# Half of a softmax-weights product moved from fp32 to three fp16 products, with the splits on three engines

## The reference

```python
q, k, v = hidden_states @ Wq, encoder_hidden_states @ Wk, encoder_hidden_states @ Wv
logits = einsum('bhqd,bhkd->bhqk', q, k) * scale + col_bias   # two masked token columns
probs = softmax(logits, axis=-1)
out = einsum('bhqk,bhkd->bhqd', probs, v) @ Wo + bo + residual
```

## Time and profile before

| | us | share of the span |
|---|---|---|
| time, median of 3 runs | 3488.54 | |
| span of the profiled execution | 3487.1 | |
| TensorE busy | 3363.5 | 96% |
| VectorE busy | 2345.2 | 67% |
| GpSimd busy | 2182.3 | 63% |
| ScalarE busy | 1765.5 | 51% |

### The profile page before, as it was taken

One profiled execution on the slowest core, in us unless ns is written; L12 is line 12 of the kernel. 1 busy time (PEld: TensorE's weight loads), 2 busy tenths in 40 slices (PEclk: granted clock), 3 DMA queues, 4 the chain that ended last, 5 costly groups with the idle time before them and its releaser, 6 DMA issues.

```text
span 3487.1 us, 70163 instructions
## 1 busy us (share of the span) xinstructions
PE 3363.5 (96%) x27442; PEld 1543.5 (44%) x27442; DVE 2345.2 (67%) x4444; ACT 1765.5 (51%) x2230; POOL 2182.3 (63%) x1050
## 2 busy tenths in 40 slices
PE   7999999999997888889999999999999999999998
PEld 3444444444442322234444444444444444444443
DVE  6666766666666788856676666666666666666666
ACT  5444444444445677764444444444444444444444
POOL 6877777767641000028777777777787677767776
PEclk9999999999998999999999999999999999999999
DMA  4000000000000000000000000000000000000000
GB/s 153 3 10 11 1 10 10 10 1 9 6 10 12 8 12 17 17 1 10 10 9 3 10 11 1 10 10 10 1 10 10 1 10 10 10 1 10 3 1 25
DMA packets 50178, 42.10 MB, mean 12 GB/s; under 512 B 4928, under 2 KB 42176, under 8 KB 49856
## 3 DMA queue, kind: packets, MB, share of 16 engines
q1 hardware_dynamic: 49136, 37.08, 3.5%
q10 hardware_dynamic: 720, 0.53, 0.1%
HBM read 32.36 MB, written 2.10 MB: 10 GB/s over the span
## 4 chain that ended last, share of the span: by engine, by line
PE 90%; ACT 3%; DVE 2%; POOL 2%; issue 2%; DMA 0%; SPq 0%; ACTq 0%; POOLq 0%; DVEq 0%
PE ps_j L858 39%; PE ps_j L1047 19%; PE ps_st L1007 13%; PE ps_sm L941 6%; PE ps_st L992 3%; PE ps_j L1034 3%; ACT pt L1495 2%; PE ps_sm L1021 2%; POOL acc L712 2%; PE ps_j L1067 1%; PE ps_st L941 1%; PE ps_j L950 1%; PE ps_j L1083 1%; PE ps_j L1058 0%; DVE nmg L1925 0%
## 5 line engine op out<-in xcount | busy, mean ns | idle before, releaser
L712 POOL TENSOR_TENSOR acc<-acc,pt 128x1024 f32<-128x1024 f32 x570 | 1365.5, 2396 | 435.8 <-ACT pt L1495 381.6
L1495 ACT ACTIVATE pt<-ps_st 128x1024 f32<-128x1024 f32 x768 | 742.7, 1019 | 447.2 <-PE ps_st L1007 435.4
L1047 PE MATMUL ps_j<-pt,v 128*64 128x512 f32 x3040 | 694.3, 599 | 1.3 <-DVE q_l L1836 1.3
L1935 DVE CUSTOM_DVE_ANT_0 ps_sm<-ps_sm,bias_m,nmx 128x512 f32<-128x512 f32 x666 | 480.5, 757 | 271.1 <-PE ps_j L941 227.5
L858 PE MATMUL ps_j<-w_h,ctx_h 128*128 128x128 f16 x3072 | 532.3, 220 | 2.3 <-ACT rinv L1511 1.1
L858 PE MATMUL ps_j<-w_l,ctx_h 128*128 128x128 f16 x3072 | 531.2, 220 | 0.0
L858 PE MATMUL ps_j<-w_h,ctx_l 128*128 128x128 f16 x3072 | 531.2, 220 | 0.0
L1935 DVE CUSTOM_DVE_ANT_0 ps_sm<-ps_sm,bias_m 128x512 f32<-128x512 f32 x486 | 334.6, 707 | 198.7 <-PE ps_j L941 185.8
L733 POOL TENSOR_TENSOR o_un<-o_un,rinv 128x512 f32<-128x512 f32 x111 | 141.7, 1277 | 477.3 <-ACT rinv L1507 293.7
L1047 PEld LDWEIGHTS ps_j<-pt,v 128*64 128x64 f32 x3040 | 201.7, 136 | 407.6 <-issue 369.6
L1972 DVE RECIPROCAL rinv<-rinv 128x256 f32<-128x256 f32 x190 | 331.4, 1746 | 14.0 <-ACT rinv L1511 4.4
(11 more groups left out here) (186 smaller groups left out, 5477.2 us busy)
## 6 DMA issues: line engine op xcount, KB each, us to landing
w_raw<-wk SPq DMA_DIRECT2D x25, 256.0 KB, 2.8
pt<-ctx_t SPq DMA_DIRECT2D x6, 1024.0 KB, 7.2
w_raw<-wv SPq DMA_DIRECT2D x24, 256.0 KB, 3.7
wo_raw<-wo SPq DMA_DIRECT2D x28, 128.0 KB, 2.0
w_raw<-wq SPq DMA_DIRECT2D x24, 128.0 KB, 2.8
k_h<-k_l SPq DMA_DIRECT2D x72, 32.0 KB, 2.0
x<-x_t SPq DMA_DIRECT2D x4, 512.0 KB, 8.3
acc<-ctx_t SPq DMA_DIRECT2D x2, 1024.0 KB, 8.4
```

What stands on the lines that cost most here:

```text
L712: G.tensor_tensor(total, first, pt[:, n % RING, :], ALU.add).then_inc(s_acc, 1)
L1047: last = MM(dst[h * HD:(h + 1) * HD, :], values_of(p)[:, kt, h * HD:(h + 1) * HD], pt[:, (units(p) + kt) % RING, h * TQ:(h + 1) * TQ], sta ...
L1495: A(pt[:, n % RING, :], src.rearrange("p h q -> p (h q)"), ACT.Exp).then_inc(s_exp, 1)
L1935: last = V.tensor_tensor_reduce(out=src, in0=src, in1=bias_m[:, t, half * HALF:(half + 1) * HALF], scale=-1.0, scalar=nmx[:, 0, t, h:h + 1 ...
```

## The change

`thirds(p)` names 78 of the 96 wide items: 4 to 28, 52 to 77 and 84 to 110 (turned slots, without those in which the x splits of a layer's start are made). For these:

- `attend_in_thirds(p)` takes the place of `attend(p, 0)`. Key tiles 0 and 1 are multiplied in fp32 as before. Key tiles 2 and 3 are three fp16 products each, V high by P high, V rest by P high, V high by P rest, for two heads: 12 fp16 matmuls in place of 4 fp32 ones (8 instructions). `attend(p, 1)` stays.
- ScalarE makes `p_h` (fp16 of P, 1024 elements a partition) twice an item, one after `queries_hi` and one between the two `keys_hi`; and the first half of V becomes two instructions of 256 elements, `v_h` (fp16, key tiles 2 and 3) and `v32` (fp32, key tiles 0 and 1).
- GpSimd makes `p_l` = P - `p_h` twice an item (`weights_rest`), one ahead of `normalize`, one behind `output_lo`.
- VectorE makes `v_l` once an item (`values_lo`) out of PSUM, between `keys_lo` 1 and the reductions of block 2.
- The next user of the PSUM bank of V waits for `v_l` too. The DMA scratch of the compiler is set to 4096 bytes; the kernel issues no DMA from GpSimd.

```diff
@@ attend_in_thirds (new; called in turned_slot when thirds(s)) @@
+                pe.wait_ge(s_exp, units(p) + 2)
+                pe.wait_ge(s_v_sb, values_before(p) + 1)
+                dst = take("pva", p)
+                for kt in range(2):
+                    for h in range(2):
+                        MM(dst[h * HD:(h + 1) * HD, :], values_of(p)[:, kt, h * HD:(h + 1) * HD],
+                           pt[:, (units(p) + kt) % RING, h * TQ:(h + 1) * TQ], start=kt == 0, stop=False)
+                pe.wait_ge(s_v_l, thirds_before(p) + 1)
+                for i in range(2):
+                    pe.wait_ge(s_p_h, 2 * thirds_before(p) + i + 1)
+                    for n, (v, w) in enumerate(((v_h, p_h), (v_l, p_h), (v_h, p_l))):
+                        if n == 2:
+                            pe.wait_ge(s_p_l, 2 * thirds_before(p) + i + 1)
+                        for h in range(2):
+                            last = MM(dst[h * HD:(h + 1) * HD, :], v[:, p % 2, i, h * HD:(h + 1) * HD],
+                                      w[:, i, h * TQ:(h + 1) * TQ], start=False, stop=i == 1 and n == 2)
+                last.then_inc(s_pva, 1)
@@ scalar engine @@
+                if thirds(p) and not half:
+                    A(v_h[:, p % 2], src[:, 2:4], ACT.Copy, scale=VS / WS)
+                    src, to = src[:, 0:2], to[:, 0:2]
+                A(to, src, ACT.Copy, scale=VS / WS).then_inc(s_v_sb, 1)
...
+            def weights_hi_of(p, i):
+                n = units(p) + 2 + i
+                act.wait_ge(s_exp, n + 1)
+                reaches(act, s_pva, wides(p))
+                A(p_h[:, i, :], pt[:, n % RING, :], ACT.Copy).then_inc(s_p_h, 1)
@@ gpsimd @@
+            def weights_rest(p, i):
+                n = units(p) + 2 + i
+                pool.wait_ge(s_p_h, 2 * thirds_before(p) + i + 1)
+                G.tensor_tensor(p_l[:, i, :], pt[:, n % RING, :], p_h[:, i, :], ALU.subtract).then_inc(s_p_l, 1)
@@ vector engine, called after keys_lo(s + 2, 1) when thirds(s + 1) @@
+            def values_lo(p):
+                dve.wait_ge(s_v_sb, values_before(p) + 1)
+                src = bank("v0", p).rearrange("p (k d) -> p k d", k=4)
+                split_lo(v_l[:, p % 2], src[:, 2:4], VS / WS, v_h[:, p % 2]).then_inc(s_v_l, 1)
@@ take @@
+                        if before == "v0" and thirds(m):
+                            pe.wait_ge(s_v_l, thirds_before(m) + 1)
```

More of the change, by code:

```diff
@@ L200, in split_sums, with thirds, thirds_before @@
     return not grouped(p) and not G0 - 3 <= p < G0
+def thirds(p):
+    return turned(p) and all(not first - 2 <= p < first + B for first in (STARTS[layer] for layer in WIDE))
+def thirds_before(p):
+    return sum(thirds(q) for q in range(p))
 def splits(p):
@@ L384, in build @@
         pt = sb("pt", [P, RING, 2 * TQ], F32)
+        p_h = sb("p_h", [P, 2, 2 * TQ], F16)
+        p_l = sb("p_l", [P, 2, 2 * TQ], F16)
+        v_h = sb("v_h", [P, 2, 2, P], F16)
+        v_l = sb("v_l", [P, 2, 2, P], F16)
         acc = sb("acc", [P, 2, 2 * TQ], F32)
@@ L460, in build @@
         s_v_sb = sem("s_v_sb")
+        s_v_l = sem("s_v_l")
+        s_p_h = sem("s_p_h")
+        s_p_l = sem("s_p_l")
         s_max_mm = sem("s_max_mm")
@@ L786, in _ @@
                     normed_lo(rms_batch(s))
+                if thirds(s):
+                    weights_rest(s, 0)
                 if past:
@@ L789, in _ @@
                     output_lo(s - 1)
+                if thirds(s):
+                    weights_rest(s, 1)
                 if summing and not turned(s):
@@ L1049, in attend, with attend_in_thirds @@
                 last.then_inc(s_pvb if part else s_pva, 1)
+            def attend_in_thirds(p):
+                pe.wait_ge(s_exp, units(p) + 2)
[15 more added lines that the diff above has]
+                last.then_inc(s_pva, 1)
             def sums(p):
@@ L1239, in turned_slot @@
                     project_out(s - 1, 0)
-                attend(s, 0)
+                if thirds(s):
+                    attend_in_thirds(s)
+                else:
+                    attend(s, 0)
                 score_block(3)
@@ L1475, in values @@
                     reaches(act, s_pvb if half else s_pva, wides(p - 2) + 1 if p >= 2 else 0)
-                A(values_of(p)[:, half * 4:half * 4 + 4, :], bank(f"v{half}", p).rearrange("p (k d) -> p k d", k=4),
-                  ACT.Copy, scale=VS / WS).then_inc(s_v_sb, 1)
+                src, to = bank(f"v{half}", p).rearrange("p (k d) -> p k d", k=4), values_of(p)[:, half * 4:half * 4 + 4, :]
+                if thirds(p) and not half:
[7 more added lines that the diff above has]
+                A(p_h[:, i, :], pt[:, n % RING, :], ACT.Copy).then_inc(s_p_h, 1)
             def exponentials(p, j):
@@ L1702, in turned_slot @@
                     queries_hi(s + 2)
-                    if not splits_x(s):
-                        keys_hi(s + 2, 0)
+                if thirds(s):
+                    weights_hi_of(s, 0)
+                if far and not splits_x(s):
+                    keys_hi(s + 2, 0)
+                if thirds(s):
+                    weights_hi_of(s, 1)
+                if far:
                     keys_hi(s + 2, 1)
@@ L2117, in turned_slot @@
                     keys_lo(s + 2, 1)
+                if thirds(s + 1):
+                    values_lo(s + 1)
                 peak()
@@ L2294 @@
     arrays["norm_w"] = np.ascontiguousarray(get("L1_xattn_norm_w").reshape(CQ, P).T)
-    nc = bacc.Bacc("TRN2", target_bir_lowering=False, num_devices=1)
+    nc = bacc.Bacc("TRN2", target_bir_lowering=False, num_devices=1, dynamic_dma_scratch_size=4096)
     a = {k: nc.dram_tensor(k, v.shape, mybir.dt.from_np(v.dtype), kind="ExternalInput").ap()
```

## The result

The changed kernel takes 3470.02 us (median of 4 runs, 3468.71 to 3470.83) against 3488.63 us of the kernel before: a ratio of 0.9949, 95% interval 0.9935 to 0.9963. That is faster by 0.5%, 18.6 us; 23.5 us were forecast, and 3470 lies inside the range. The profiled execution has a span of 3468.4 us and a time of 3470.16.

A forecast was written before the change was run, and what follows sets the result against it. TensorE's list of work was taken to bound every wide slot. Terms of -33.5, +8 and +2 us sum to -23.5 us, taking the span from 3487.1 to 3463.6 and the median to 3465 us, range 3453 to 3487.

The forecast's parts named there:

- The bound: In wide slots, TensorE's list of work sets the length: it is busy 30.03 of 30.03 us.
- Term 1: First half of P V on TensorE: 3.59 to 3.16 us, -0.43 us an item, x 78 = -33.5 us.
- The five waits: Semaphore waits inside the new TensorE function: met early, costed at nothing, bounded by 0.1 us an item, 8 us.
- ScalarE: Two copies of P, 1.06 us each, hidden in 1.99 us waits; V in two parts 0.68 us, complete 0.08 us later.
- Term 2: VectorE's rest of V delays a block 2 reduction and the closing pair's second head: +0.10 us x 78 = +8 us.
- Term 3: Six slots where VectorE builds token rows: slower rest of P delays normalize and VectorE, 6 x 0.33 = +2 us.
- Cover lost: From GpSimd's first rest of P on, every further 0.1 us goes straight through o_h and V.
- rival 2: Slow first rest of P on GpSimd: gain gone from about 2.5 us on; at 3.0 us, 3529 us; chance 0.12.
- GpSimd goes from 21.6 to 25.9 us in a slot of 29.7: full, but no bound: GpSimd's work in a slot with two rests of P added: fuller, but not what sets the slot's length.
- wrong altogether: Signs in the trace against the whole prediction: TensorE waiting for p_l, for o_l, or for an exponential.
- Rival 1: VectorE's queue ahead of the closing pair costs much more than 0.1: 0.35 us a slot, 3484 us; chance 0.20.
- Rival 3: TensorE's half-array fp16 products do not hide weight loads: six loads add 0.6 us, 3512 us; chance 0.06.

The follow-up runs named there:

- the products alone: Changed kernel with split tiles zeroed once at the start, the splits in the slots and their waits left out: 3454.34 us, 0.9905 of the kernel before.
- the splits alone: Changed kernel with all splits made, but the first half of P V in fp32 again and ScalarE copying all of V: 3516.3 us, 1.0085 of the kernel before.
- the addition ahead of the normalization: Changed kernel plus an unused GpSimd subtraction of 192 elements between the first rest of P and the normalization: 3495.95 us, 1.0027 of the kernel before.
- the rest of V moved: Changed kernel with VectorE's rest of V between the two reductions of block 2 instead of ahead of them: 3458.41 us, 0.9919 of the kernel before.
- both edits: Changed kernel with item 110 left unsplit and the rest of V placed between the two reductions of block 2: 3456.4 us, 0.991 of the kernel before.

## Why the prediction was right, and where not

- **The number**: 18.6 us of the 23.5 forecast. The sum of the plain slots was right to 0.01 us a slot. What is missing in the profiled execution is slot 110 (4.4 us with its own share of the gain), slot 28 (1.1), four slots with 0.13 each (0.5), the slots where the splits begin (0.3) and the clock in layer 1 (1.0); the higher clock at the start gave 2.5 back. That last one is luck: by its own slots the change gave 17.3 us.
- **The bound**: right. TensorE's list sets a wide slot; the slot fell with it.
- **Term 1, -0.43 us an item**: right. 3.59 to 3.16 us in the trace, 0.42 a slot with the products alone. The five waits cost nothing.
- **ScalarE**: right. The two copies of P took 1.05 us each inside waits for TensorE; V in two parts took 0.66 us (0.68 assumed, 0.70 as an estimate from the figures of the Trainium skill, which stand in the section What ACT_TABLE_LOAD costs of ScalarE: Activation LUTs, not in the one that the prediction names).
- **Term 2, +0.10 us**: right in place and size. Moving one instruction on VectorE removed it; the splits alone, with 0.22 us more on ScalarE, gave 0.32.
- **Term 3**: the place was right, the size a little high: the six token slots lost 0.24 us more than plain ones, 0.33 were assumed, 1.4 us in place of 2. Without the rests of P they lost nothing.
- **"Cover lost: from the first rest on, every further 0.1 us goes straight through"**: too strict. V had 0.16 us to spare, because neighbours on ScalarE overlap and `normalize` was 0.23 us late in the slot (1988.25 - 1973.82 against 1997.96 - 1983.76), not 0.30. That is why 0.50 us brought 0.34, and it puts rival 2's point at a rest of about 2.6 us.
- **"GpSimd goes from 21.6 to 25.9 us in a slot of 29.7: full, but no bound"**: this step failed, for one slot in 78. It was worked out from a plain slot and carried over to all ("all 78 items have this slot", and the only exceptions that it goes on to name are the six token slots), but slot 110 has no Q and K projections; there GpSimd was the bound before the change already, and was given 2.1 us more, with a fall of the clock behind the wait. It gave back 4.1 us of a forecast 23.5. The row was to be had: TensorE's wait of 2.30 us for `o_l` at 3445.27. TensorE waiting for `o_l` is one of the prediction's own signs of being wrong altogether, and it came in this one slot. The 21.6 is a slip besides: the slot of the earlier trace rows has 20.97, and with two rests of 2.13 that makes 25.2; 25.06 was measured.
- **Rival 1** (0.3 us or more on VectorE) and **rival 2** (GpSimd): neither came true, and the splits only and the addition ahead of the normalization show that both mechanisms are real: 0.5 us more a slot on GpSimd made the kernel 0.3% slower than the one before (1.0027). **Rival 3** is out, with different weights in each half array: steps of 0.215 us. Each of the six pairs of loads lies beside the products before it. The rule named with it (TensorE: Matmul & The Clock Gate, The mechanism, in the Trainium skill), that a load overlaps only when its row group differs, does not hold in this trace. The same section also lets a load that goes to the background weight buffer run ahead of running matmuls, and that sentence the trace fits.
- One smaller loss was not tested by itself: in slot 28 VectorE's two splits of the Q weights of layer 1, from SBUF, took 3.79 us in place of 2.98, and the slot 0.81 more. Without the rests of P they took 2.98 again. Slots 12 and 56 show the same with another split (2.92 in place of 1.70). It fits that GpSimd's additions, which the rests move in time, hold these instructions up; that it is the additions is not shown.

## What to carry to other kernels

When all work is counted against one full engine, the price of side work is read at the one or two starts where it meets that engine's list: here a semaphore that one reduction gives, with 0.34 us to spare. Place the new instruction behind the one that gives it, not ahead of it: that move alone was worth about 10 us here (28.9 us under the kernel before in place of 18.6). And look at the first and last slots by themselves before multiplying: where the bound engine has less to do, the cover is gone.

## What was not expected of the hardware

TensorE's granted clock can fall behind a wait of a few microseconds. Behind the wait in slot 110 each profiled execution had this clock, as a mean over a stretch of 7 us, from 3.1 us ahead of the end of the wait to 3.9 behind it:

| wait | clock, kernel |
|---|---|
| 4.9 us | 0.76 (more ahead of the normalization) |
| 4.4 us | 0.59 (the changed kernel), 0.63 (splits only), 0.76 (the rest of V moved) |
| 2.3 us | 0.76 (item 110 without the split), 0.79 (the rests of P left out), 1.00 (the kernel before, both edits, products only) |

So it fell in all four executions with the longer wait and in two of five with the shorter. A wait near the end can cost twice: 2.1 us of waiting more brought 4.1 us, the rest being fp32 steps of 0.87 us where 0.43 is usual, which is the lower of the two levels.

The clock also explains where executions differ far from the change. The start of the program (to 120 us) ranged over 3.1 us, and the stretch of layer 1 over 4.3 us, among the ten profiled executions; the start was short at a granted clock of 1.00 and long at 0.96, and the places of layer 1 looked at were long at 0.94. What makes the clock fall there in one execution and not in another was not followed. Each kernel was profiled once, so how much of the spread of a median comes from these places is not shown.
